# A four-layer sequence kernel: other due times for the same pieces of work on TensorE, ScalarE, VectorE, GpSimd and the DMA queue

## The reference, cut to what matters

```python
x = L0(x, t)            # norm over all of (S, D), FiLM scale/shift, SiLU, @ W_in, the same norm again, @ W_out, + x
x = L1(x, mask, step, bias)   # AdaLN, 16-head attention with a full bias and a mask, @ Wo, then 256 -> 1024 -> 256 with GELU
x = L2(x, A, B, dt)     # stencil: first and second differences along both axes, max(x + df * dt, 0)
x = L3(x, gate)         # 16-head causal attention and 256 -> 1024 -> 256 with GELU, gated residual
```

## Time and profile before

| what | value |
|---|---|
| median of three executions | 2571.6 us |
| the profiled execution's own time | 2576.85 us |
| its span, first to last instruction | 2575.5 us |
| TensorE (PE) busy | 2455.6 us, 95% |
| ScalarE (ACT) busy | 2110.1 us, 82% |
| VectorE (DVE) busy | 1977.3 us, 77% |
| GpSimd (POOL) busy | 1539.3 us, 60% |
| mean granted TensorE clock | 0.981 |
| DMA | 287.58 MB, 112 GB/s on average |

### The profile page before, as it was taken

How to read it: one execution, slowest core, us unless ns; L and a number is a source line. 1 busy time by engine, 2 the same in 40 slices (tenths; PEclk the granted TensorE clock), 3 DMA queues, 4 the chain that set the end, 5 groups by cost and what they waited for, 6 DMA issues and landing times.

```text
span 2575.5 us, 57162 instructions
## 1 busy us (share of the span) xinstructions
PE 2455.6 (95%) x19136; PEld 2003.3 (78%) x19136; DVE 1977.3 (77%) x7387; ACT 2110.1 (82%) x4694; POOL 1539.3 (60%) x1487
## 2 busy tenths in 40 slices
PE   6878999999999999999999999999999999999997
PEld 5666788888878888887888888788888888877776
DVE  6776777888787787878778887877888787778653
ACT  2556888888888888888888888888888888888775
POOL 2556665655766665576666557666565766655421
PEclk6799999999999999999999999999999999999999
DMA  5433444434444443344444343444434344433311
GB/s 207 122 120 102 122 120 119 114 101 109 110 126 121 120 112 104 107 108 126 121 122 111 105 109 105 126 122 122 111 103 112 103 126 122 128 103 98 84 30 34
DMA packets 141667, 287.58 MB, mean 112 GB/s; under 512 B 33792, under 2 KB 37888, under 8 KB 141120
## 3 DMA queue, kind: packets, MB, share of 16 engines
q1 hardware_dynamic: 141376, 283.92, 40.1%
HBM read 174.64 MB, written 8.45 MB: 71 GB/s over the span
## 4 chain that ended last, share of the span: by engine, by line
PE 78%; ACT 11%; DVE 5%; POOL 3%; issue 2%; DMA 1%; SPq 1%; POOLq 0%; DVEq 0%; ACTq 0%
PE bank L1452 18%; PE bank L1530 17%; PE bank L1553 11%; PE bank L1568 7%; PE bank L1512 7%; PE bank L1543 6%; ACT PB L1254 4%; PE bank L1464 3%; PE bank L1519 3%; PE bank L1706 2%; PE bank L1578 2%; ACT BB L1274 1%; ACT AA L1280 1%; ACT BB L1280 1%; DVE smt L989 1%
## 5 line engine op out<-in xcount | busy, mean ns | idle before, releaser
L1254 ACT ACTIVATE PB<-PB,mx 128x256 f32<-128x256 f32 (+1 forms) x2048 | 844.1, 476 | 35.8 <-DVE mx L1011 34.7
L580 POOL TENSOR_TENSOR BT<-BT,MN 128x1024 f32<-128x1024 f32 x256 | 555.9, 2185 | 74.4 <-DMA BT<-in_bias 73.8
L1553 PE MATMUL bank<-ident,PB 128*128 128x128 f32 x3584 | 483.6, 274 | 6.9 <-ACT PT L1259 3.2
L1011 DVE CUSTOM_DVE_ANT_0 PB<-bank,BT 128x256 f32<-128x256 f32 x1024 | 373.3, 420 | 122.1 <-PE bank L1543 118.2
L1553 PEld LDWEIGHTS bank<-ident,PB 128*128 128x128 f32 x3584 | 421.2, 141 | 57.9 <-ACT PB L1254 11.5
L1452 PE MATMUL bank<-TN,WS_w 128*128 128x256 f16 x3072 | 379.9, 274 | 42.7 <-ACT BB L1280 22.8
L1018 DVE COPY PT<-bank 128x512 f32<-128x512 f32 (+1 forms) x512 | 316.1, 617 | 89.3 <-PE bank L1553 89.1
L1452 PEld LDWEIGHTS bank<-TN,WS_w 128*128 128x128 f16 x3072 | 286.0, 98 | 122.9 <-ACT AA L1280 39.7
L1543 PE MATMUL bank<-Ks,Qs 96*128 96x512 f32 (+1 forms) x1024 | 359.6, 428 | 13.9 <-DVE mx L1011 8.6
L1011 DVE CUSTOM_DVE_ANT_0 PB<-bank,caus 128x128 f32<-128x128 f32 (+1 forms) x1024 | 303.3, 352 | 69.9 <-PE bank L1543 69.7
L1259 ACT ACTIVATE PT<-bank 128x512 f32<-128x512 f32 (+1 forms) x512 | 272.7, 533 | 72.8 <-PE bank L1553 72.8
(11 more groups left out here) (282 smaller groups left out, 4654.8 us busy)
## 6 DMA issues: line engine op xcount, KB each, us to landing
BT<-in_bias SPq DMA_DIRECT2D x256, 512.0 KB, 4.5
Qs<-QX SPq DMA_DIRECT2D x256, 128.0 KB, 2.7
Ks<-KX SPq DMA_DIRECT2D x512, 64.0 KB, 2.4
Qs<-QX SPq DMA_DIRECT2D x256, 64.0 KB, 2.6
Ks<-KX SPq DMA_DIRECT2D x512, 32.0 KB, 2.2
XT<-in_xT SPq DMA_DIRECT2D x32, 256.0 KB, 5.2
X<-in_x SPq DMA_DIRECT2D x32, 256.0 KB, 3.0
AB<-ada_rows SPq DMA_DIRECT2D x32, 256.0 KB, 3.8
```

Of the source, the lines that this page charges most:

```text
L580: G.op.tensor_tensor(v2(BT[k % 4]), v2(BT[k % 4]), MN[:, :].unsqueeze(1).broadcast_to([128, 2, 512]), ALU.add).then_inc(g_bt, 1)
L1011: V.op.tensor_tensor_reduce(PB[(2 * D + q) % 6][:, h * 256:h * 256 + w], bS[q][:, h * w:h * w + w], plus, -1.0, 3.0e38, ALU.add, ALU.min, ...
L1254: S.op.activation(o, o, ACT.Exp, scale=-1.0, bias=mx[u.layer][:, c:c + 1]).then_inc(a_exp, 1)
L1553: last = T.op.transpose(bP[h][:, c * 128:c * 128 + 128], PB[(2 * u.D + q) % 6][:, h * 256 + k * 128:h * 256 + k * 128 + 128], ident[:, :])
```

## The change

Only the numbers in `P`, `OWN` and `SPLIT` change, some 430 of them, most by 1 to 10 ticks. No instruction is added or removed (15202 matmuls on TensorE in both, 6887 rows on VectorE), no wait, no buffer. A few lines of it:

```diff
 P = {
-    "score0": -1, "score1": -1, "bias0": 0, "bias1": 0, "exp0": 2, "exp1": 3, "flip0": 8, "flip1": 8, "ev0": 7,
-    "ev1": 9, "pv": 14, "cx": 14, "ct": 17, "pvn": 17, "ld_bt": -13, "mask_add": -26, "stack": -6, "ld_x": -71,
+    "score0": -1, "score1": 0, "bias0": 0, "bias1": 0, "exp0": 2, "exp1": 4, "flip0": 8, "flip1": 8, "ev0": 9,
+    "ev1": 9, "pv": 14, "cx": 14, "ct": 17, "pvn": 17, "ld_bt": -8, "mask_add": -24, "stack": -3, "ld_x": -71,
...
 SPLIT = {
-    "bias1_3": 0, "exp0_3": 2, "exp1_3": 3, "ev0_3": 8, "ev1_3": 10, "pv_3": 13, "cx_3": 13, "ct_3": 17, "pvn_3": 18,
-    "stack_3": -7,
+    "bias1_3": 1, "exp0_3": 2, "exp1_3": 3, "ev0_3": 8, "ev1_3": 10, "pv_3": 13, "cx_3": 13, "ct_3": 16, "pvn_3": 18,
+    "stack_3": 2,
 }
```

More of the change, by code:

```diff
@@ L56 @@
 P = {
-    "score0": -1, "score1": -1, "bias0": 0, "bias1": 0, "exp0": 2, "exp1": 3, "flip0": 8, "flip1": 8, "ev0": 7,
-    "ev1": 9, "pv": 14, "cx": 14, "ct": 17, "pvn": 17, "ld_bt": -13, "mask_add": -26, "stack": -6, "ld_x": -71,
-    "ld_xn": -41, "ld_ab": -37, "ld_mask": -85, "mask": -31, "n1_stats": -70, "n1_ones": -68, "n1_sum": -67,
[6 rows of a table removed]
-    "f1": 73, "s_pm": 59, "s_b": 60, "s_r": 74, "s_rp": 81, "s_re": 97, "s_ha": 74, "s_w": 98, "s_ab": 98,
-    "s_row": 101, "s_mm": 103, "s_f": 104, "ld_w1": -24, "ld_sten": -46, "ld_w3": -277, "coefs": -21,
+    "score0": -1, "score1": 0, "bias0": 0, "bias1": 0, "exp0": 2, "exp1": 4, "flip0": 8, "flip1": 8, "ev0": 9,
+    "ev1": 9, "pv": 14, "cx": 14, "ct": 17, "pvn": 17, "ld_bt": -8, "mask_add": -24, "stack": -3, "ld_x": -71,
+    "ld_xn": -38, "ld_ab": -62, "ld_mask": -63, "mask": -33, "n1_stats": -73, "n1_ones": -66, "n1_sum": -67,
[6 rows of a table added]
+    "f1": 74, "s_pm": 63, "s_b": 69, "s_r": 74, "s_rp": 80, "s_re": 97, "s_ha": 89, "s_w": 97, "s_ab": 100,
+    "s_row": 108, "s_mm": 104, "s_f": 106, "ld_w1": -24, "ld_sten": -46, "ld_w3": -277, "coefs": -21,
     "split_p1": -55, "split_p1_hi": -50, "split_p1_lo": -45, "split_w1": -8, "split_w1_hi": -4, "split_w1_lo": -2,
     "split_p3": 46, "split_p3_hi": 50, "split_p3_lo": 54, "split_w3": 82, "split_w3_hi": 88, "split_w3_lo": 92,
[4 rows of a table removed]
-    "st_out": 83,
[4 rows of a table added]
+    "st_out": 95,
 }
@@ L91 @@
     -2: {
[6 rows of a table removed]
-        "m1": 50, "t2_lo": 60, "f1": 80, "s_r": 82, "s_rp": 90, "s_re": 91, "s_ab": 99, "s_f": 112, "m3": -46,
[9 rows of a table removed]
[6 rows of a table added]
+        "m1": 52, "t2_lo": 60, "f1": 79, "s_r": 80, "s_rp": 92, "s_re": 97, "s_ab": 97, "s_f": 103, "m3": -46,
[8 rows of a table added]
+        "ld_ab": -30, "ld_mask": -16, "ld_bt_1": 3, "stack_1": 3, "s_row": 110, "stack_3": -16, "st_out": 751,
     },
     -1: {
[6 rows of a table removed]
-        "t2_lo": 70, "f1": 86, "s_r": 90, "s_rp": 93, "s_re": 97, "s_ab": 98, "s_f": 101, "m3": -54, "t3_lo": -39,
[7 rows of a table removed]
-        "m4_b": 734, "ld_x": -100, "ld_xn": -68, "ld_ab": -27, "ld_mask": -100, "ld_bt_1": -14, "stack_1": -12,
-        "stack_3": 273, "st_out": 1017,
-    },
[17 rows of a table removed]
-        "y3": -33, "m4_rstd": 33, "m4_b": 55, "scr": -390, "ld_mask": -325, "ld_sten": -150, "ld_ab": -181,
-        "ld_w1": -71, "ld_w3": -93, "ld_bt_1": 0, "stack_1": 0, "s_row": 103, "stack_3": -13, "st_out": 89,
-    },
[7 rows of a table removed]
-        "t2_lo": 63, "f1": 80, "s_r": 80, "s_rp": 85, "s_re": 94, "s_w": 97, "s_ab": 97, "s_f": 101, "m3": -50,
[7 rows of a table removed]
-        "ld_mask": -31, "ld_ab": -41, "ld_bt_1": -8, "stack_1": -1, "s_row": 91, "stack_3": -13, "st_out": 75,
[6 rows of a table added]
+        "t2_lo": 72, "f1": 84, "s_r": 91, "s_rp": 94, "s_re": 97, "s_ab": 97, "s_f": 100, "m3": -58, "t3_lo": -39,
[7 rows of a table added]
+        "m4_b": 745, "ld_x": -61, "ld_xn": -67, "ld_ab": -24, "ld_mask": -136, "ld_bt_1": 6, "stack_1": 10,
+        "stack_3": 262, "st_out": 1012,
+    },
[17 rows of a table added]
+        "y3": -35, "m4_rstd": 39, "m4_b": 52, "scr": -463, "ld_mask": -395, "ld_sten": -140, "ld_ab": -180,
+        "ld_w1": -45, "ld_w3": -72, "ld_bt_1": -19, "stack_1": -18, "s_row": 97, "stack_3": -3, "st_out": 94,
+    },
[7 rows of a table added]
+        "t2_lo": 58, "f1": 82, "s_r": 83, "s_rp": 86, "s_re": 94, "s_w": 95, "s_ab": 98, "s_f": 103, "m3": -55,
[7 rows of a table added]
+        "ld_mask": -53, "ld_ab": -33, "ld_bt_1": -2, "stack_1": 5, "s_row": 105, "stack_3": 1, "st_out": 86,
     },
```

## The result

The changed kernel takes 2607.83 us (median of four runs, 2605.47 to 2613.58) against 2571.12 us before: a ratio of 1.0142, 95% interval 1.0122 to 1.0162. It is slower by 36.7 us; 2576.0 was forecast, and 2588 was the upper end. The profiled execution has a span of 2612.3 us, 36.8 above that of before.

What follows compares the result with a forecast made beforehand. TensorE was taken to set the 75.05 us period; terms of +0.40 a period, 24 times, gave +9.6, less 5.2 in the ends, so +4.4 on the median 2571.6: 2576.0 us, range 2561 to 2588.

Steps and rivals of the forecast that it cites:

- (e): Two GpSimd operations of 1.27 us come ahead of `smt`, making it late: +0.10 us a period, bounds 0 and 0.39.
- (a): Scores behind `pv` on TensorE cost 0.10 us extra at each of two new places: +0.20 a period, bounds 0 and 0.20.
- (b): Nine score pairs split into single scores on TensorE: 0 a period, bounds -0.09 and +0.09 us.
- (c): One 128x512 score leaves the held gaps of the `w1` chain: +0.23 us a period, bounds 0 and 0.23.
- (d): ScalarE copies before `ev0` in the `w3` chain, first pitch 2.41 instead of 2.54: -0.13 us a period, or 0.
- the ends: Three TensorE waits shrink, two in the head (-1.7, -2.1) and one in the tail (-1.4): -5.2 us together.
- (f): DMA queue: three more issues, 1.8 us in all, ahead of layer 1's second stack, first used 7.7 later: 0.
- R2: Rival: GpSimd becomes late in full, 0.39 instead of 0.10 a period: 2583.0 us, chance 0.16.
- R1: Rival: scores behind `pv` cost nothing extra: 2571.2 us, chance 0.14.
- R4: Rival: lone scores are cheaper than halves of a pair, -0.9 us a period: 2554.4 us, chance 0.06.
- everything else: All other moves on ScalarE and VectorE have slack around them (116 and 180 us idle of 900): 0.
- R3: Rival: the ends give much more, the head's whole 9.00 us wait and score waits: 2561.4 us, chance 0.15.

Runs made afterwards that it cites:

- e1: Changed kernel with the output store (st_out) at tick 83 instead of 95, ahead of layer 1's first stack again: ratio 1.0099, period 75.99 us.
- e13: Changed kernel with st_out at 83 and s_b at 66 instead of 69, so GpSimd's L626 stands ahead of the last bias block: ratio 1.0057.
- e3: Changed kernel, store still late, with GpSimd's m1_b back at 32 and q3_lo at -23 (L618 ahead of bias blocks, L565 behind smt): ratio 1.0532.
- e8: Changed kernel with the store at 83 and GpSimd's m1_b at 32 and q3_lo at -23: ratio 1.0134.
- e14: Changed kernel with the store at 83 and score1 at -1 instead of 0, so that scores stand in pairs again: ratio 1.0105.
- f11: Kernel before with ev0 at 9 instead of 7 and win_out at -39 instead of -40, w3 copies ahead of ev0: ratio 1.0020, period 75.08 us.
- e16: Changed kernel with st_out at 83, s_b at 66 and the first batch's v1_out at -115 instead of -132: ratio 1.0017.
- f6: Kernel before with three first-batch numbers moved (n2_scale -230, n2_gate -228, split_p1_lo -226), scales of the first weights made earlier: ratio 0.9992.
- f13: Kernel before with f6's three numbers and the last batch's t4 at 326 instead of 340: ratio 0.9995.

## Why the prediction was wrong

What a period lost, by the runs, against what the text had:

| term | forecast | measured | from |
|---|---|---|---|
| store late behind the stack | 0 | 0.56 | 76.55 - 75.99 (e1) |
| `smt` late, (e) | 0.10 (up to 0.39) | 0.47 | 75.99 - 75.52 (e13) |
| (a), (b), (c), (d) and the rest | 0.30 | 0.47 | 75.52 - 75.05 |
| sum | 0.40 | 1.50 | |

The two late inputs were taken away one after the other. With the late store in place TensorE's wait for `smt` is 0.27 a period (6.4 us), without it 0.40, so that part of (e) is hidden in the changed kernel. Of the 32.3 us between the forecast's +4.4 and the measured +36.7 the store is some 13, `smt` 9, the other terms of the period 4 and the ends 6.

**(f), the step that failed most.** The text priced three issues that came ahead of a stack, asked when that stack is first used, and put 0. One of the three was the store, and the text never asked who waits for the store itself. It was named as something that delays and not as something that is delayed: it had moved behind the first stack of layer 1, which is issued only when GpSimd has made the low parts of q and k. Its waiter is two batches later in the same buffer, through ScalarE, at `t3`. e1 takes 0.43% back by this one number, e3 shows the same wait grow to 60.8 us when the queue ahead of the store slips.

It is the time of the issue that did it. Before, the landing took longer (median 4.3 us, up to 5.7) and TensorE did not wait for it, because the store was issued 34.6 us behind `win` (median) and the normalisation came at 47.2; in the changed kernel it is issued at 45.7. Most of the variation of the periods comes with it: over the 24 periods the landing took 2.3 to 4.5 us, and in the five where it took over 4 us TensorE waited 1.39 to 1.82. e13's periods are equal but one.

**(e), the place was right, the sum was not.** The text added 2.54 us of moved work and took off the idle 2.15. But one idle stretch was not free: the last bias block starts when its transfer lands. Work ahead of it is absorbed, work behind it is not. Only L626 (1.27) had moved behind it, into 0.69 of slack. The bound of 0.39 was from the wrong sum and too low; e8 shows that the two operations on which the text put the blame were better off where the change put them, given the order of the other engines. R2, the rival with this mechanism, had the direction and too small a price.

**(a) was right.** e13's rows at one of the two new places, the other has the same distances:

```profile
1116.66 0.86 PE L1568 MATMUL bank<-PT,VW 128*32 128x256 f32 x16
1117.44 0.50 PE L1543 MATMUL bank<-Ks,Qs 96*128 96x512 f32 x1
1117.79 1.49 PE L1452 MATMUL bank<-HB,WS_p 128*128 128x256 f16 x12
1119.03 0.48 PE L1543 MATMUL bank<-Ks,Qs 96*128 96x512 f32 x1
1119.34 0.82 PE L1553 MATMUL bank<-ident,PB 128*128 128x128 f32 x6
```

From `pv` to q3 it is 1.13 with the score between them, and 0.79 before, without one: the score costs 0.34. From q3 to the flips it is 1.56 (median of the periods), and twelve with flips behind take 1.32: the same score costs 0.24 there. That is 0.10 for the place behind `pv`, 0.21 for both. R1 falls. The reading of the Trainium skill, "TensorEngine Tiling (Array Packing)", Key Properties, that would have made it nothing falls with it: the number of changes of mode is the same in both orders and the time is not. What in the hardware takes the 0.10 the runs do not show.

**(b) was right**: two single scores at 0.24 are the pair's 0.47, at this and the other places between twelve and flips. R4 falls with it. **(c) was right**: TensorE's wait for `AA` is 0.81 a time in e13 (19.5 us in 24) and 0.58 before, 0.23 more, because the score that used to fill it is elsewhere. e14, where that score is back, has 0.58 again. **(d) was right in place and size for the changed kernel** (14.3 us of waiting for `BB` instead of 17.3), but f11 shows that it is worth nothing by itself in the kernel before. Together 0.21 + 0.23 - 0.13 = 0.31, where the runs leave 0.47. The difference of 0.16 has a row that covers it and more, in e13:

```profile
1104.43 0.36 PE L1543 MATMUL bank<-Ks,Qs 96*128 96x256 f32 x1
1104.83 0.42 PEld L1519 LDWEIGHTS bank<-ident,AA 128*128 128x128 f32 x4 [0.24 <-ACT AA L1274]
```

Ahead of `t2` one score stands where two stood. The second had covered ScalarE's normalisation; the load of `t2`'s first tile now waits 0.24 for it, 5.7 us in 24 periods. Some of this comes back at places that were not listed. The text gave "everything else" 0 because ScalarE and VectorE have slack. The slack of an engine says nothing of a wait that a neighbour on TensorE had covered.

**The ends.** -5.2 was forecast; they came out at +0.9. The three waits shrank (9.00 to 4.92, 2.13 to 1.16, 1.42 to none, where 7.3, none and none were written), and the last is worth what the text said. The first is not worth its wait: other waits came up around it, and the head's own order gives 0.3 to 1.1 us and not 1.7. And a fourth row, L1100, which the text did not price, had moved ahead of the work that had filled its wait, and gave back more. With that mended and the store early (e16) the ends are 7 to 8.5 us better than before. That is some of what R3, the faster rival, promised, but not by its mechanism, since 4.92 of the 9.00 stay and the first period is no shorter; which of the other numbers made it was not followed up. It could not decide, since the period loses 36.

## What to carry to other kernels

When an order changes, list for every transfer that moved in a queue not only what it delays but who waits for its landing, through buffers too: a store is an input of whoever writes its buffer next. In a stretch with a gate in it (a landing, a release), idle time ahead of the gate absorbs only work ahead of the gate; count what moved to behind it separately. And an order is one thing over all engines: TensorE's order of before was 2.3 us a period slower than the changed one when set among the changed orders of the others (78.89 against 76.55).

## What was not expected of the hardware

The granted clock of the first 100 us differed between runs with nearly the same work there. Busy time by stretch, the kernel before, then f6, then f13:

```profile
0.00:100.00 100.00, 71.14 (x352) 57.22 (x352) 68.06 (x227) 29.50 (x56) 35.51 (x41) 0.68 0.56 183
```

```profile
0.00:100.00 100.00, 72.35 (x394) 57.80 (x395) 71.14 (x244) 33.72 (x66) 38.58 (x43) 0.74 0.61 199
```

```profile
0.00:100.00 100.00, 71.44 (x380) 57.52 (x380) 68.89 (x236) 32.19 (x62) 36.18 (x42) 0.73 0.59 192
```

The first `win`, four matmuls, took 3.75 us before and 1.97 in f6, the two levels of 1.2 and 2.4 GHz. f13 has the same head as f6, number for number, and its `win` took 3.37, in part at the lower level; its sixth `win` starts at 376.7 us and that of f6 at 372.1. So 4.6 us of a head differ between two profiles of one order, and a gain of that size cannot be read from a single profile of each kernel.
